# Window attention and convolution on one core: scores from two groups of 64 rows, with plain and spread stacks for queries and keys

## The reference

```python
x = x + _L0_conv_ref(_gn(x), ...)      # gating, qkv, attention in 8x8 windows, projection
x = x + _L1_conv_ref(_gn(x), ...)      # 3x3 convolution
```

```python
g = (x * ac_w[None, :, None, None] + ac_b[None, :, None, None]) * x
g = jnp.clip(g, 0.0, 6.0)
qkv = jnp.einsum('bchw,dc->bdhw', g, qkv_w)
...
attn = jnp.einsum('wnqd,wnkd->wnqk', q, k) * scale
attn = jax.nn.softmax(attn, axis=-1)
o = jnp.einsum('wnqk,wnkd->wnqd', attn, v)
...
out = jnp.einsum('bchw,dc->bdhw', o, proj_w) + proj_b[None, :, None, None]
```

## Time and profile before

| what | us |
|---|---|
| median of 3 runs | 1663.28 |
| lowest and highest | 1657.38, 1670.82 |
| profiled execution, own time | 1678.25 |
| its span, first to last instruction | 1676.5 |
| PE busy | 1296.1 (77% of the span) |
| DVE busy | 1005.9 (60%) |
| ACT busy | 782.4 (47%) |
| POOL busy | 380.2 (23%) |

### The profile page before, as it was taken

How to read it: one execution, slowest core, us unless ns; L and a number is a source line. 1 busy time by engine, 2 the same in 40 slices (tenths; PEclk the granted TensorE clock), 3 DMA queues, 4 the chain that set the end, 5 groups by cost and what they waited for, 6 DMA issues and landing times. The chain is left out here.

```text
span 1676.5 us, 57125 instructions
## 1 busy us (share of the span) xinstructions
PE 1296.1 (77%) x23523; PEld 854.3 (51%) x23523; DVE 1005.9 (60%) x1379; ACT 782.4 (47%) x1107; POOL 380.2 (23%) x245
## 2 busy tenths in 40 slices
PE   1388787887878888597874888888889888859876
PEld 0166565555655666433322656656656666643332
DVE  7555445454544454399994555455654565439998
ACT  3545444444544453344432545454544465435443
POOL 5001111111111110255551111111111111025665
PEclk9778768887887797599995888788985799859998
DMA  5223222232322231012232322332322233200111
GB/s 221 76 91 108 79 75 92 81 90 82 108 83 82 81 115 48 1 55 96 100 130 98 117 85 92 93 95 83 118 83 80 89 113 98 66 2 38 50 50 63
DMA packets 113491, 142.86 MB, mean 85 GB/s; under 512 B 19440, under 2 KB 89584, under 8 KB 112240
## 3 DMA queue, kind: packets, MB, share of 16 engines
q1 hardware_dynamic: 113264, 139.31, 26.1%
HBM read 70.06 MB, written 69.21 MB: 83 GB/s over the span
## 5 line engine op out<-in xcount | busy, mean ns | idle before, releaser
L457 ACT ACTIVATE work<-ps,ws 128x1024 f32<-128x1024 f32 x256 | 285.0, 1113 | 490.4 <-PE ps L886 485.9
L668 DVE TENSOR_REDUCE m_all<-ps 128x16 f32<-128x1024 f32 x256 | 311.9, 1219 | 181.1 <-PE ps L873 179.2
L904 PEld LDWEIGHTS ps<-v_ext,work 128*64 128x64 f32 x8192 | 320.2, 158 | 81.6 <-ACT work L457 64.8
L904 PE MATMUL ps<-v_ext,work 128*64 128x18 f32 x8192 | 328.7, 225 | 39.4 <-ACT work L457 30.2
L873 PE MATMUL ps<-k_stack,q_stack 96*64 96x256 f16 x2048 | 190.3, 315 | 162.7 <-DMA k_stack<-stack_scratch 93.7
L372 POOL TENSOR_TENSOR g_lo<-work,g_hi 128x512 f16<-128x512 f32 x64 | 74.2, 1159 | 1003.0 <-ACT g_hi L493 1003.0
L873 PEld LDWEIGHTS ps<-k_stack,q_stack 96*64 96x64 f16 x2048 | 107.5, 123 | 269.1 <-issue 252.9
L886 PEld LDWEIGHTS ps<-q_stack,k_stack 128*64 128x64 f16 x8192 | 178.4, 124 | 75.6 <-issue 75.3
L886 PE MATMUL ps<-q_stack,k_stack 128*64 128x64 f16 x8192 | 205.2, 209 | 4.6 <-issue 4.2
L836 PE MATMUL ps<-work,c_hi 128*128 128x512 f16 x384 | 152.2, 396 | 68.4 <-DVE work L756 68.3
L681 DVE TENSOR_TENSOR work<-ps,work 128x512 f16<-128x512 f32 x64 | 44.3, 692 | 242.3 <-ACT work L475 242.3
(11 more groups left out here) (125 smaller groups left out, 1660.3 us busy)
## 6 DMA issues: line engine op xcount, KB each, us to landing
stack_scratch<-work SPq DMA_DIRECT2D x128, 256.0 KB, 2.1
q_stack<-stack_scratch SPq DMA_DIRECT2D x64, 384.0 KB, 3.9
k_stack<-stack_scratch SPq DMA_DIRECT2D x256, 96.0 KB
stack_scratch<-work SPq DMA_DIRECT2D x128, 128.0 KB, 2.1
out_dram<-work SPq DMA_DIRECT2D x32, 512.0 KB, 2.7
img<-in_x_dram SPq DMA_DIRECT2D x8, 1024.0 KB, 14.2
img<-in_x_dram SPq DMA_DIRECT2D x16, 512.0 KB, 3.8
max_scratch<-m_pair SPq DMA_DIRECT2D x64, 32.0 KB, 1.8
```

The costliest lines, as they stand in the source:

```text
L457: a.activation(probs[:, p % 2, :], ps[:, ST_B:ST_B + 2, :].rearrange("p w t -> p (w t)"), ACT.Exp, scale=ws[:, R_EXP:R_EXP + 1]).then_inc( ...
L668: v.tensor_reduce(m_all[:, 0, :, p, :], ps[:, S_B:S_B + 2, :].rearrange("p h (g j k) -> p (h g) j k", g=2, k=WIN), AX.X, ALU.max).then_inc ...
L904: mm = t_.matmul(ps[64 * w:64 * w + 64, PV_B + p // 2, col:col + VC], probs[:, p % 2, at:at + WIN], v_ext[:, md, 2 * p + w, hp, :], start= ...
```

## The change

A stack now has two heads instead of four (48 rows), and two stacks lie on the two halves of the partitions: rows 0 to 47 and rows 64 to 111 (`HR` = 2 row groups, `HG` = 4 stacks in each, `HJ` = 2 heads in a stack). Every score matmul uses 64 x 64 of the array.

Both products now have a plain and a spread operand of their own: `scores` takes plain queries `q_pl` and spread keys `k_bd`, `scores_t` takes plain keys `k_pl` and spread queries `q_bd`. Both make 16 matmuls of 128 moving columns per pair. So queries and keys are each read back twice. The stacks are two buffers deep (`TWO`), the scratch in memory three. Two rows in each half of `q_bd` take the maxima; the matching rows of `k_pl` hold -4096. The maxima still go through memory, now one write and two reads. The mask on ACT at the start (`mask4`, four instructions) goes.

The order of the work changes too. The key projection moves to the head of the iteration, in bank GB, and `v_rows` goes to bank GA. `output` moves behind `weigh(n-1, 2)`. On ACT the copies of the values stand ahead of `g_hi` and `exps(n, 0)`, and `turned` is one copy of 512 columns. The loop body holds `TURN` = 6 iterations. The core of the diff:

```diff
-HG, HJ = 4, 4
+HR, HG, HJ = 2, 4, 2
 ...
+TWO = 2
+TURN = 6
 ...
-        q_stack = sb("q_stack", [P, BUFS, HG, UT], F16)
-        k_stack = sb("k_stack", [P, BUFS, HG, HJ, UT], F16)
+        q_pl = sb("q_pl", [P, TWO, HG, UT], F16)
+        k_bd = sb("k_bd", [P, TWO, HG, HJ, UT], F16)
+        k_pl = sb("k_pl", [P, TWO, HG, UT], F16)
+        q_bd = sb("q_bd", [P, TWO, HG, HJ, UT], F16)
 ...
+                    def plain(to, src, event):
+                        rows = src.rearrange("(r g a) s t -> r (a s) g t", r=HR, g=HG)
+                        for r in range(HR):
+                            sp.dma_start(to[64 * r:64 * r + ROWS, :, :], rows[r]).then_inc(event, 16)
+                    def spread(to, src, event):
+                        rows = src.rearrange("(r g j d) s t -> r j (d s) g t", r=HR, g=HG, j=HJ)
+                        for r in range(HR):
+                            for j in range(HJ):
+                                at = 64 * r + HROWS * j
+                                sp.dma_start(to[at:at + HROWS, :, j, :], rows[r, j]).then_inc(event, 16)
 ...
+                    if "B" in on:
+                        after(sp, qd_in, n)
+                        after(sp, kd_in, n)
+                        write(n + 2, 1)
+                        write(n + 2, 0)
+                        after(sp, kc_in, n + 1)
+                        after(sp, qc_in, n + 1)
+                        after(sp, k_sent, n + 2)
+                        after(sp, s_done, n)
+                        spread(k_bd[:, m % TWO, :, :, :], stackd[(m + 2) % BUFS, 1], kc_in)
+                        after(sp, q_sent, n + 2)
+                        plain(q_pl[:, m % TWO, :, :], stackd[(m + 2) % BUFS, 0], qc_in)
+                    if "C" in on:
 ...
+                        after(sp, st_done, n + 1 - TWO)
+                        spread(q_bd[:, (m + 1) % TWO, :, :, :], stackd[(m + 1) % BUFS, 0], qd_in)
+                        plain(k_pl[:, (m + 1) % TWO, :, :], stackd[(m + 1) % BUFS, 1], kd_in)
 ...
+                        for g in range(HG):
+                            for w in range(2):
+                                tok = slice((2 * p + w) * WIN, (2 * p + w + 1) * WIN)
+                                for r in range(HR):
+                                    rows = slice(64 * r, 64 * r + ROWS)
+                                    mm = t_.matmul(ps[64 * w:64 * w + 64, S_B + r, g * P:g * P + P],
+                                                   q_pl[rows, (m + 1) % TWO, g, tok], k_bd[rows, (m + 1) % TWO, g, :, tok],
+                                                   start=True, stop=True)
 ...
+                            for g in range(HG):
+                                h, c = g // 2, g % 2
+                                for r in range(HR):
+                                    rows = slice(64 * r, 64 * r + ROWS + 2)
+                                    at = w * 256 + h * P
+                                    mm = t_.matmul(ps[64 * c:64 * c + 64, ST_B + r, at:at + P],
+                                                   k_pl[rows, md % TWO, g, tok], q_bd[rows, md % TWO, g, :, tok],
+                                                   start=True, stop=True)
```

242 lines of the change are left out of this document (106 added, 136 removed).

## The result

The changed kernel takes 1824.88 us (median of 4 runs, 1820.78 to 1888.94), the kernel before 1664.78 us beside it (4 runs, 1657.38 to 1670.82). The ratio is 1.0956, with a 95% interval from 1.0897 to 1.1015. The forecast was 1481 us and "faster"; the kernel is slower by 9.6%, above the upper end of the range and above rival 3 too. The profiled execution spans 1822.8 us at a mean granted clock of 0.648, against 1676.5 us and 0.828 before.

A forecast was written before the change was run, and what follows sets the result against it. PE, idling for keys and partly at low clock, bounds the old kernel; SP's reads would bound the new. 0.75 x 14.2 + 0.25 x 17.1 + 0.4 = 15.3 us against 18.27, times 62, scaled: 1481 us; range 1355 to 1616.

The forecast's parts named there:

- rival 3: SP's key write waits behind slow reads, deciding from 14.5 us: iteration 19.0 us, kernel slower at 1708 us; chance 0.13.
- I take 25%: PE clock: share of time at the lower level, down from 36% as idle time falls from 2 to 0.7 us.
- The 15.55 us of the iteration: Old loop at full clock: 13.5 us from scores through the maxima transpose, then 2.04 us idle waiting for keys.
- rival 2: PE clock stays low throughout because quarter matmuls are lighter work: 17.5 us per iteration, 1616 us; chance 0.12.
- 3.6 us more: Extra PE work in a low-clock iteration: 16.50 us at clock 0.76 against 12.86 us at 1.00.
- The order on ACT: Value copies and `g_hi` between exponentials of pairs 3 and 0: 1.8 us against `weigh` and `scores_t`, costed at 0.4 us.
- The matmuls: Quarter-array scores and `scores_t` on PE save 1.3 us per iteration, bounds 0 and 2.6 us.
- PE's own cycle of 13.5 us: PE's new full-clock iteration: 13.5 - 1.3 + 0.5 + 0.4 + 0.4 us, between 12.2 and 14.8; hardly changed.
- The 0.5 us for `output`: `output` ends just before pair 3's `scores_t`; ACT's 0.78 us scaling precedes that exponential, about 0.5 us not covered.
- the 0.4 us for the switches of shape: PE array-shape switches: seven more per iteration, four not behind a wait, 0.1 us each.
- SP and the reads: SP's queue, key write to key write with twelve reads, sets the iteration at 14.2 us, bounds 12.8 and 18.6.
- The turn of the loop: Loop body of six: 8 turns for 16, each costing 3.1 us, 25 us in all, 0.4 us per iteration.

The follow-up runs named there:

- rows_104: Kernel before with `scores_t` over the 104 rows that hold something instead of all 128: 1708.18 us, ratio 1.0204 to the kernel before.
- rows_64: Changed kernel with both score products over all 64 rows of a group, the added rows zeros in one operand: 1813.98 us, 1.0804 to the kernel before.
- projections_twice: Changed kernel with each query and key projection computed twice, six matmuls more per iteration: 1802.19 us, 1.0717 to the kernel before.
- filler_8: Changed kernel plus one dense, overwritten matmul ahead of each group of scores and `scores_t`, eight per iteration: 1767.04 us, 1.0508 to the kernel before.
- copies_later: Changed kernel with value copies behind `g_hi` and pair 0's exponential, PE's first output transpose behind `scores_t` of pair 1: 1716.10 us, 1.0222 to the kernel before.
- before_body_6: Kernel before with a loop body of six iterations for three: 1657.20 us, 0.9878 to the kernel before.
- quarters_filled: `copies_later` plus eight dense matmuls of constants ahead of scores and `scores_t`: 1643.11 us, kernel before 1673.10 us beside it; too spread for a ratio.
- order_filler_8: Kernel before with only the new order (old stacks, halves of the array), plus eight dense matmuls per iteration: 1768.28 us, 1.0555 to the kernel before.

## Why the prediction was wrong

*The gain that was forecast was never in the full clock.* The earlier trace rows had an iteration of the kernel before at 14.00 us and clock 1.00, and the prediction gave the new one 14.2 us. So by its own numbers nothing was to be had there (the ten intervals between transposes at clock 1.00 in the kernel before take 13.9 to 15.3 us); the 2.97 us came from the iterations at the lower level, from "I take 25%" and "13.5 + 3.6 = 17.1 us". The 15.55 us of the iteration hid that.

*The clock: the step that failed.* The prediction tied the lower level to idle time alone ("with the idle time down from 2 us to 0.7 us I take 25%"). The wait ahead of the scores did go, PE's idle time as a whole fell from 3.1 to 2.6 us only, and the clock in the loops, 0.56 and 0.58, puts 84 to 88% of the time at the lower level. `rows_104` (zeros left out, 2.0% slower) and `rows_64` (zeros added, 1.4% faster) show that the rows in use count, and `projections_twice` and `filler_8` that added dense work can shorten the kernel. The rows are a small part of it: filled up, they leave the clock at 0.661. What holds it down for the rest, the fewer columns that each matmul streams or the waits between them, no run separates. Rival 2 named lighter matmuls as the mechanism, and its sign of "clock under 0.75" came; it was given 0.12. The Trainium skill (TensorE: Matmul & The Clock Gate, What's actually happening) says that the clock is set by how busy the engine has been lately. If busy means busy time as the profile counts it, this case doesn't agree: PE is busy for 541 of 620 us against 477 of 584 and the clock fell. The low clock lengthens the busy time itself, so the clearer case is `copies_later`, where PE is busy for 19.16 of 20.10 us at clock 0.50.

*The price of the low clock, mis-sized.* "3.6 us more" was read from an iteration at clock 0.76, which is about half the time at each level. At levels nearer to 0.50 PE's busy time rises by 7.9 us in the old form (`before_body_6`, 13.05 to 20.91 at clock 0.60) and by 6.1 us in `copies_later` (13.06 at 0.85 to 19.16 at 0.50). With rival 2's own base that is 13.5 + 7 = 20.5 us, which is what nearly every iteration took. The match is partly luck, since PE is busy for 18.28 of these 20.53 us and waits for the rest; rival 2's 1616 was low by this term and by the next. The sheet of before could have told it: with 36% of the time low, 14.0 us in the others and a mean of 18.27, the low iterations had to be far over 17 us, turns of the loop included.

*The order on ACT, mis-sized.* By what undoing it gives back, 7.3 of the 9.6 points, this is no smaller miss than the clock. The copies and `g_hi` between the exponentials were seen and costed at 0.4 us ("1.8 us of ACT against `weigh` and `scores_t`"). What was missed is what the copies wait for: `v_ext` has three buffers, so they need `weigh` of pair 3 of the iteration at hand to be over. The 1.8 us do not lie beside `weigh`, they come behind it, with the exponential and PE's next `weigh` behind them. Measured near the full clock: 2.45 us (16.46 against 14.01). In time, moving them took 1.0956 to 1.0222, with the mean clock nearly as low as before, 0.656. About half of what that gave back is PE's idle time and half its busy time; why the busy time fell at the same mean clock was not looked into.

*The matmuls.* The groups of scores were to take 0.45 to 0.55 us; they take 0.42 at the full clock and 0.64 at the low one. `scores_t` takes 0.42 for 0.69 at the full clock. Four times 0.21 + 0.27 is 1.9 us of durations, for 1.3 taken and bounds of 0 and 2.6. This term was within its bounds and 0.6 us better than taken. PE's own cycle of 13.5 us was too high rather than too low at the full clock: 14.01 us in `quarters_filled`, less 8 x 0.22 us of added matmuls, is 12.3 us by estimate, with the copies moved. The 0.5 us for `output` and the 0.4 us for the switches of shape no run took apart.

*SP and the reads.* 14.2 us as the bound did not come, but nothing contradicts it as an upper value: `quarters_filled` runs at 14.01 us. In the attention SP's waits are led by `m_pair` and not by `qd_in` or `kd_in`, against the sign promised. The DMA share of 0.47 met "about 0.5". Rival 3 had the right side, slower, by the wrong mechanism: its reads need 11.5 us and not over 14.5, SP waits for ACT, and doubled plain reads cost 1.5%.

*The turn of the loop.* Priced at 3.1 us. In the changed kernel a turn lengthens its iteration by 26.2 - 20.5 = 5.7 us in the first phase, and 23.9 - 20.5 = 3.4 us in the second, which is near the price. In `order_filler_8` it is 24.68 - 17.25 = 7.4 us, and PE's busy time rises by 4 us in it at clock 0.79, so about half of this turn's price is the lower clock in it. The body of six was worth 1.2% to the kernel before (1677.98 - 1657.20 = 21 us; the prediction's 3.1 us for 8 turns saved is 25 us), so it probably helped in the changed kernel too, and hid a part of the loss. The Trainium skill (Runtime: NRT & Kernel Launch, Instruction fetch mechanics) names a stall at a taken branch, without a price; the 5.7 and 3.4 us are this case's.

Taken together: the kernel is slower because PE runs at the low level for over 84% of the loop, and because the value copies stand in series with `weigh`. The second is worth 7.3 points when it is undone alone; the first shows in added matmuls taking 1.0956 to 1.0508, and in `copies_later` at 1716.10 us against `quarters_filled` at 1643.11 us (the kernel before took 1681.43 and 1673.10 us beside them). The two act on each other and their shares don't add. Still open is why the clock falls, beyond the 1.4 to 2.0% that the rows in use make.

## What to carry to other kernels

Where TensorE's clock moves between its two levels, don't assume that cheaper matmuls and less idle time raise it. Price an iteration at each level from rows whose clock is near 0.5 and near 1.0, and test a suspected fall with a kernel that only adds rows of zeros or a matmul of constants. When a step is moved on an engine, look up first what it waits for: a copy that waits for a buffer delays everything queued behind it. Compare the forecast of the new iteration with the best iteration of the old kernel; if they are equal, the whole forecast rests on how often the best one occurs.

## What the runs showed of the hardware

- Rows of zeros change the clock: 24 rows left out of `scores_t`, 2.0% slower, clock 0.794 for about 0.83; rows filled up to 64, 1.4% and 1.7 points faster, clock 0.661 for 0.648 and 0.879 for 0.843.
- PE can be busy for 19.16 of 20.10 us, three times in a row, and stay at clock 0.50 (`copies_later`, 233.69 to 294.01).
- Added matmuls shorten a kernel: six per iteration, 1.0956 to 1.0717; eight, to 1.0508; four in idle time of the kernel before, to 0.9812.
- At low clock 16 quarter matmuls of 128 columns took 0.64 us and at full clock 0.42 us, for 1.06 and 0.63 us of eight halves of 256 columns: the eight halves, two at a time, stream 8 x 256 / 2 = 1024 columns, which is 0.43 us at 2.4 GHz and leaves 0.20 us. With the same 0.20 us four quarters at a time, 16 x 128 / 4 = 512 columns or 0.21 us, make 0.41 us, and at 1.2 GHz 0.43 + 0.20 = 0.63 us. Both fit, so by this estimate four quarters run beside each other, and the constant part keeps the gain under a half.
- The turn of the loop body: for the kernel before, a body of 24 for one of three took 1681.43 - 1604.76 = 77 us off for 14 of its 16 passes, 5.5 us each; a body of six took 21 us off for 8 passes, 2.6 us each. What made the first eight cheaper was not looked for.
